# Two-layer mixer kernel: the decay copies go from ACT to POOL, and all calls are placed anew

## What is computed

```python
def step(S, inp):                      # layer 0's mixer, 256 steps, 16 heads of 8x8
    qt, kt, vt, at, bt = inp
    Sk = einsum('bhde,bhe->bhd', S, kt)
    S_new = at * S - at * bt * (Sk x kt) + bt * (vt x kt)
    return S_new, einsum('bhd,bhde->bhe', qt, S_new)
# q, k, v: silu(depthwise conv of 4 taps(silu(x W + b))), q and k of unit norm;
# a, b: sigmoid(x W + b)
# layer 0's feed-forward: 8 experts of 128 -> 512 -> 128, top 2 by a router
# layer 1's mixer: a decayed, normalised prefix sum; its feed-forward: 128 -> 512 -> 128
#   between butterfly maps, with a GELU
x = x + ga * mixer(layernorm(x) * (1 + ca) + sa)
x = x + gb * feed_forward(layernorm(x) * (1 + cb) + sb)
```

## Time and profile before

| | |
|---|---|
| median of 3 runs | 560.04 us (558.86 to 561.19) |
| the profiled execution | 558.77 us; its span, first to last instruction, 557.0 us |
| busy, share of the span | PE 448.9 us (81%), DVE 331.7 (60%), ACT 391.8 (70%), POOL 144.3 (26%) |
| mean granted clock of PE | 0.940 |
| HBM | 13.78 MB read, 1.05 MB written, 27 GB/s over the span |
| table loads on ACT | 41 at L1119, 31 at L1117, 3 at L1350 |

### The profile page before, as it was taken

One profiled execution on the slowest core, in us unless ns is written; L12 is line 12 of the kernel. 1 busy time (PEld: TensorE's weight loads), 2 busy tenths in 40 slices (PEclk: granted clock), 3 DMA queues, 4 the chain that ended last, 5 costly groups with the idle time before them and its releaser, 6 DMA issues.

```text
span 557.0 us, 6629 instructions
## 1 busy us (share of the span) xinstructions
PE 448.9 (81%) x2090; PEld 304.8 (55%) x2090; DVE 331.7 (60%) x741; ACT 391.8 (70%) x690; POOL 144.3 (26%) x176
## 2 busy tenths in 40 slices
PE   3667695766859858799798999999999999977167
PEld 2555582645646636566576565677565666643022
DVE  2305968582689752899889779789323293110920
ACT  5676878876676784968947887656896874964243
POOL 1130452308021474008481012342003000011001
PEclk9879997997979979899999999999999999999679
DMA  7636595005620023440221800000000000000000
GB/s 190 235 111 162 182 356 121 2 1 133 167 64 2 1 67 85 101 113 1 61 61 32 211 2 20 1 1 0 1 0 21 1 1 1 0 12 6 0 1 19
DMA packets 34321, 35.44 MB, mean 64 GB/s; under 512 B 12776, under 2 KB 30320, under 8 KB 34032
## 3 DMA queue, kind: packets, MB, share of 16 engines
q1 hardware_dynamic: 34000, 30.84, 21.1%
q10 hardware_dynamic: 288, 4.19, 2.0%
HBM read 13.78 MB, written 1.05 MB: 27 GB/s over the span
## 4 chain that ended last, share of the span: by engine, by line
PE 48%; ACT 26%; DVE 8%; POOL 7%; issue 7%; POOLq 0%; DVEq 0%; ACTq 0%
PE psF L756 13%; PE psS L774 13%; ACT L1117 4%; PE psB L713 4%; ACT L1119 3%; ACT hid L1313 3%; PE psM L587 3%; PE psM L817 2%; ACT hS L1162 2%; PE psM L824 2%; ACT sq L1147 1%; ACT h L1162 1%; PE psM L626 1%; ACT sq L1149 1%; DVE psT L1877 1%
## 5 line engine op out<-in xcount | busy, mean ns | idle before, releaser
L774 PEld LDWEIGHTS psS<-we2s,hid 128*128 128x128 f32 x1024 | 135.9, 195 | 55.1 <-issue 42.9
L756 PE MATMUL psF<-h,we1s 128*128 128x512 f32 (+1 forms) x320 | 140.2, 530 | 20.2 <-ACT hid L1313 15.0
L774 PE MATMUL psS<-we2s,hid 128*128 128x128 f32 x1024 | 138.3, 279 | 3.8 <-ACT hid L1313 2.0
L1313 ACT ACTIVATE hid<-psF,col 128x512 f32<-128x512 f32 (+1 forms) x160 | 93.3, 598 | 60.9 <-PE psF L756 60.3
L756 PEld LDWEIGHTS psF<-h,we1s 128*128 128x128 f32 x320 | 56.1, 199 | 48.6 <-issue 24.0
L2277 POOL TENSOR_TENSOR QS<-H,qn 128x256 f32<-128x256 f32 x64 | 51.6, 827 | 97.6 <-DVE H L1887 76.0
L1900 DVE SCALAR_TENSOR_TENSOR acc<-psS,gate,acc 128x128 f32<-128x128 f32 x128 | 36.2, 342 | 51.3 <-PE psS L774 47.5
L1887 DVE TENSOR_TENSOR_SCAN H<-A,psT 128x320 f32<-128x320 f32 x64 | 52.5, 820 | 3.9 <-ACT A L1253 1.7
L1119 ACT ACT_TABLE_LOAD x41 | 52.6, 1283 | 1.4 <-PEq L2434 0.7
L1877 DVE TENSOR_TENSOR psT<-wrep,H 128x360 f32<-128x360 f32 x64 | 39.9, 623 | 2.2 <-DMA wrep<-XX 1.0
L1117 ACT ACT_TABLE_LOAD x31 | 39.8, 1283 | 0.5
(11 more groups left out here) (198 smaller groups left out, 668.5 us busy)
## 6 DMA issues: line engine op xcount, KB each, us to landing
wrep<-XX SPq DMA_DIRECT2D x72, 160.0 KB, 3.4
krep<-kn SPq DMA_DIRECT2D x64, 128.0 KB, 2.5
hid<-fold_mats_dram SPq DMA_DIRECT2D x22, 256.0 KB, 5.3
we1s<-we_dram ACTq DMA_DIRECT2D x1, 2048.0 KB, 9.3
we2s<-we_dram ACTq DMA_DIRECT2D x1, 2048.0 KB, 16.5
outT_dram<-x SPq DMA_DIRECT2D x4, 256.0 KB, 3.0
M<-mats_dram SPq DMA_DIRECT2D x1, 576.0 KB, 5.3
x<-xT_dram SPq DMA_DIRECT2D x2, 256.0 KB, 6.8
```

The source lines that it names most:

```text
L756: mm(bank[name][:, 0:ncols(w)], we1s[:, e, k * P:(k + 1) * P], h2[w % 2][:, 0:ncols(w)], start=True, stop=True).then_inc(s_hid_mm, 1)
L774: last = mm(bank[name][:, t * P:(t + 1) * P], hid[n % 2][:, k, t * P:(t + 1) * P], we2s[:, e, k, :], start=(k == 0), stop=(k == HT - 1))
L1313: nc.scalar.activation(hid[x_ % 2][:, k, 0:c], psF[n % 2][:, 0:c], ACT.Silu, bias=pc("be1", HT * e + k)).then_inc(s_hid_done, 1)
```

## The change

`decays` moves from ACT's program to POOL's. What it waits for and what waits for it stay the same; the activation with Copy becomes POOL's tensor copy. POOL's list asks for copies up to about six chunks ahead of the chunk that is scanned. The lists of all engines are written in a new order; their calls are the same ones. The number of fills stays at 23.

```diff
 @block.scalar
-            def decays(w, i):
-
-                g = chunks(w)[i]
-                h, c = i // CPH, i % CPH
-                if i == 0:
-                    act.wait_ge(s_gates_done, 2 * (w + 1))
-                if g - NA + 1 > 0:
-                    act.wait_ge(s_scan_done, g - NA + 1)
-                a = hbt(ag[w % 2][:, 0:ncols(w)])[:, h, :, c * CH:(c + 1) * CH].unsqueeze(1).broadcast_to([P, DH, NB, CH])
-                nc.scalar.activation(A9[g % NA][:, :, :, 1:], a,
-                                     ACT.Copy).then_inc(s_a9_done, 1)
 @block.gpsimd
+            def decays(w, i):
+
+                g = chunks(w)[i]
+                h, c = i // CPH, i % CPH
+                if i == 0:
+                    pool.wait_ge(s_gates_done, 2 * (w + 1))
+                if g - NA + 1 > 0:
+                    pool.wait_ge(s_scan_done, g - NA + 1)
+                a = hbt(ag[w % 2][:, 0:ncols(w)])[:, h, :, c * CH:(c + 1) * CH].unsqueeze(1).broadcast_to([P, DH, NB, CH])
+                g_.tensor_copy(A9[g % NA][:, :, :, 1:], a).then_inc(s_a9_done, 1)
 @block.sync, the list
             loads()
-            fold_load(9)
-            fold_load(10)
-            fold_load(8)
             spread_keys(0)
+            fold_load(8)
             spread_solved(0)
+            fold_load(10)
+            fold_load(9)
 @block.tensor, the list
-            modulation()
             square_sums(0)
+            modulation()
 @block.gpsimd, the list
             keys(0)
+            for i in range(0, 7):
+                decays(0, i)
             read_state(0, 0)
+            decays(0, 7)
+            read_state(0, 1)
```

More of the change, by code:

```diff
@@ L892, in _ @@
-            slot(0, 22)
+            fill(9)
+            project(3, 2)
+            slot(0, 23)
             attn_out(1)
[L894 to L898, removed]
+            slot(0, 24)
+            slot(0, 25)
+            center(("moe", 1))
+            project(3, 3)
+            variance(("moe", 1))
+            slot(0, 26)
+            project(3, 4)
+            for s in range(27, 31):
                 slot(0, s)
-            project(3, 3)
@@ L954, in _ @@
[L954 to L960, removed]
[L961 to L968 removed]
+            slot(2, 7)
+            experts_back(1)
+            gate_rows(2)
@@ L969, in _ @@
+            slot(2, 8)
+            center(("ssd", 0))
+            router_bias(2)
+            slot(2, 9)
+            slot(2, 10)
+            variance(("ssd", 0))
+            slot(2, 11)
+            fill(22)
+            square_sums(4)
+            slot(2, 12)
+            fill(13)
+            slot(2, 13)
+            attn_out(4)
+            for s in range(14, 18):
+                slot(2, s)
             ssd_in(0)
-            for s in range(15, 20):
-                slot(2, s)
             key_products(4, 0)
@@ L1020, in _ @@
             center(("moe", 4))
-            fill(21)
-            slot(3, 23)
-            slot(3, 24)
+            for s in range(22, 25):
+                slot(3, s)
             variance(("moe", 4))
@@ L1027, in _ @@
             ssd_out(1)
-            for s in range(27, 30):
-                slot(3, s)
+            slot(3, 27)
             center(("ffn", 1))
+            slot(3, 28)
+            slot(3, 29)
             router(4)
@@ L2050, in _ @@
             carry_hf(2)
+            convolve(1)
             ln(("front", 2))
-            convolve(1)
-            for i in range(0, 4):
-                chunk(0, i)
+            chunk(0, 0)
+            chunk(0, 1)
             carry(2)
-            for i in range(4, 8):
+            for i in range(2, 8):
                 chunk(0, i)
@@ L2128, in _ @@
             ln(("ssd", 0))
-            chunk(3, 9)
+            for i in range(8, 11):
+                chunk(3, i)
             mix_expert(2, 1)
-            for i in range(10, 13):
-                chunk(3, i)
+            chunk(3, 11)
+            chunk(3, 12)
             mix_expert(2, 2)
-            for i in range(13, 16):
-                chunk(3, i)
+            chunk(3, 13)
+            couple(4, 0)
+            chunk(3, 14)
+            couple(4, 1)
+            chunk(3, 15)
+            mix_expert(2, 3)
@@ L2163, in _ @@
             mix_expert(3, 2)
-            ln(("ssd", 1))
-            for i in range(13, 16):
-                chunk(4, i)
+            chunk(4, 14)
+            chunk(4, 15)
             ssd_decay(1)
@@ L2343, in _ @@
+            decays(3, 12)
+            read_state(3, 6)
+            read_state(3, 7)
+            keys(4)
+            decays(3, 13)
+            decays(3, 14)
+            for i in range(8, 11):
+                read_state(3, i)
+            decays(3, 15)
+            read_state(3, 11)
+            decays(4, 0)
+            decays(4, 1)
+            read_state(3, 12)
+            attn_residual(4)
+            for i in range(13, 16):
                 read_state(3, i)
-            attn_residual(4)
```

780 lines of the change are left out of this document (373 added, 407 removed).

## The result

| | before | changed |
|---|---|---|
| median of the first comparison, us | 560.21 (558.86 to 561.19) | 553.72 (552.30 to 553.85) |
| ratio | 1 | 0.9863 [0.9823, 0.9903] |
| repeated with more runs, us | 561.53 | 552.67, ratio 0.9848 [0.9811, 0.9885] |
| profiled execution, span | 557.0 | 551.8; repeated 549.8 |

The change is faster by 1.4 to 1.5%, about 8 us by the ratios; the medians of the first comparison are 6.5 us apart. All ratios are to the kernel before, run on the same chip in turn. They and these medians use the undisturbed executions alone: of 23 of the kernel before in the repeated comparison, three took 567.6 to 649.4 us, at lower clocks, and are left out.

What follows compares the result with a forecast made beforehand. No engine was full: before 240 us work waits for work, afterwards PE and DVE are nearly full. Terms -1.3 + 1.3 + 1.0 - 2.5 - 3.8 + 0.5 = -4.8 took 560.0 to 555.2 us; own range 551 to 558, wider 546 to 563.

Steps and rivals of the forecast that it cites:

- Copies off ACT: Removing 64 copies from ACT saves the 1.3 us they hold on the chain: -1.3 us.
- Copies on POOL: Copies at 0.70 us each stand ahead of awaited read-outs in stages 2 and 3: +1.3 us, bounds 0 and +2.7.
- DVE against POOL: More POOL work slows the product that begins each scan chunk on DVE, through shared SBUF access: +1.0 us.
- Rival 1: POOL's copies collide with DVE's first products in half of 64 chunks, 12.8 us on DVE: 567 us, chance 0.12.
- Stage 0: Square sums and norms go before the modulation; keys 5.2 us earlier, key products 3.2: -2.5 us, bounds 0 and -5.2.
- Long stretches: Before 240 us, three more expert slots fill each of two ACT stretches, for one more table load: -3.8 us.
- Late stretch: From 390 us on, two more table loads switching between Gelu and Silu at 1.28 us each: +0.5, bounds 0 and +2.6.
- Tests stated ahead: Forecast wrong if PE idle before 240 us shrinks under 3 us, scans wait over 2, or first product's mean exceeds 0.70.
- Rival 4: Scans wait for POOL's copies, 1.2 us in each of five stages: 561 us, chance 0.06.
- Rival 2: Gains are hidden because DVE's scans set when PE's stages start: no change, 559.5 us, chance 0.22.

Runs made afterwards that it cites:

- e6: Changed kernel with no copies at all, scan tiles filled once with a constant: ratio 0.9836 to the kernel before, against 0.9848 for the changed kernel.
- the halves of the order: Without copies, against the kernel before: new order only up to stage 2's solve and keys, 0.9995; new order only from there on, 0.9954.
- e10: No copies; calls up to stage 2's solve and keys (about 137 us) in the new order, the rest old: ratio 0.9995 to the kernel before.
- Experiment 7: Changed kernel with PE and ACT put back in the old order from about 120 to 160 us: ratio 0.9991 to the kernel before.

## Why the prediction was right, step by step

The forecast of 555.2 us was 1.5 us above the measured 553.72. It was right in sign, in rough size, and in that the gain is made before 240 us. But its terms were mostly wrong, and what made the gain was not among them. That the sum came out near is luck: by the ratios the gain is 7.7 to 8.5 us, against 4.8.

- *Copies off ACT, -1.3*: not contradicted in the old order, 0.8 us (no copies: 0.9985 [0.995, 1.002]). In the new order it is the largest single term: on ACT the copies would cost 6.6 to 9.4 us more than on POOL. The step that failed reads the copies' worth from the chain of before and applies it to another order.
- *Copies on POOL, +1.3, at 0.70 us each*: mis-sized. The median copy took 0.40 us (386 to 763 ns), near ACT's 0.408, and POOL was 24.9 us busier and not 45. The Trainium skill's line rate (GPSIMD Engine Reference, Engine selection) made it an estimated 0.21 us; the trace shows twice that, and its conclusion of a term near 0 held in the new order (0.7 us, no copies: 0.9836 against 0.9848). In the old order the place named cost more than the term: 2.25 us more waiting and 1.7 us of slow matmuls. The new order has read-outs and projections in other places, and there the chain does not pass through them.
- *DVE against POOL, +1.0*: right only by chance. The first product's mean rose from 623 to 639 ns, 16 ns by 64 is 1.0 us of DVE time. But the kernels without any copy have 647 ns in the new order and 653 in the old one, and with 64 copies on POOL it is 646 (changed, repeated) and 654. So the copies add nothing to it that these traces can tell; one execution differs from another by more. Nor did the row of the prediction show quite what it was read for: the product at 67.30 started 0.5 us ahead of the multiply shown in the earlier trace rows and 0.2 us behind the one before it (67.12, 0.73 us). By the Trainium skill (SBUF - State Buffer, SBUF: two separate sides) the two engines lock each other out for a whole instruction; the trace agrees in that the copy at 226.38, which started 0.03 us behind a first product of 0.54 us, took 0.76 us where 0.39 was the least of all, but few copies met one. Rival 1, 12.8 us of collisions, fell.
- *Stage 0, -2.5*: the keys came at 31.24, as predicted. The key products came at 39.53 and not near 37, because the first projection of stage 1 waited for ACT's modulation (0.79 us at 37.65), which waits for the modulation matmuls that the change puts later, and the products for ACT's p (0.73 us). The lead did not reach the end in the kernel before (1.0007), where the fold's loads moved with it.
- *Long stretches, -3.8*: wrong. Their shape came as described: no stall of PE there is over 4 us, where 6.51 and 5.19 had been. But the norms that the path goes through ended hardly sooner (the load behind them is at 127.20 in the first profile and at 125.38 in the second, against 126.40 before), and the ACT part of the move alone cost 5.1 us. The step counted slots gained for PE, which was not what the next stage waited for. (Three slots at 1.1 us are also 3.3 us, not 3.2.)
- *Late stretch, +0.5*: nothing to be seen; behind the keys of stage 4 both spans have 285 us left.
- *Missing*: the projections of stage 3 ahead of the attention's output, and the router behind its slots. The order excerpts that I had looked at stopped short of these calls. Undoing them, with what moves along, costs the full 7 to 8 us. This is the step that the prediction left out: it took the row from the attention's output over the projections of stage 3 and ACT's modulation to the router as given, and this row was the path.
- *Tests stated ahead*: ACT was 16.3 us less busy instead of 24, for the reason in the last section. The scans' waits of 5.2 us crossed my limit of 2 us, by which the forecast was to be called wrong. They did no harm, since without them (e6) only 0.7 us is won. PE's idle time before 240 us shrank by 8.7 us in the first profile, more than the 3 asked for. Rival 4's price was too high for the same reason. Rival 2 (hidden anyway) fell by the ratio.

What stays open is why the halves of the order give so much less apart than together. The granted clock has a part in it that I did not separate. From 60 to 120 us it was 0.88 and 0.83 (two stretches of 30 us) in e10, and 0.96 and 0.93 in the kernel with the whole new order, for nearly the same calls. Experiment 7 moves several calls at once; their shares were read from its trace and not run apart.

## What to carry to other kernels

A move between engines and a new order must be priced together: here the engine alone was 2.5 us slower, the order alone at best 1.9 us faster, and both 8 us faster, because in the new order the copies would stand on the path of the engine that the move relieves. The worth of a wait is not its length: follow what the next stage's first instruction waits for, through queues of other engines as well. Here ACT's queue set both the router's start on PE and DVE's convolution, behind which the scans stood. The excerpt of the order that you price must cover the whole row that the chain runs through. An engine's hole that is there anyway (PE waiting for keys) is a good place for work whose readers are on another engine.

## What the runs showed of the hardware

- ACT's instructions overlap. 64 copies of 408 ns are 24.3 us of busy time, but leaving them all out takes only 17.9 us off ACT (391.8 to 373.9), 0.28 us each; the chain charges 0.30 to 0.31.
- The same 16 matmuls of the attention's output took 3.72 us behind 0.72 us of idle, 3.72 us behind 3.20 us of idle, both at a clock of 1.00, and 5.41 us behind 2.97 us of idle, at a clock of 0.68. What decides between the last two was not found.
- Executions of the very same kernel before, on which the ratios rest, went from 558.2 to 564.8 us, with mean granted clocks of 0.942 down to 0.920; ten of the changed kernel kept within 551.6 to 553.9. With such a spread, ratios from six to twelve runs carry 0.2 to 0.4% each way, and the marks of a single profile 2 us.
